# One graph, mixing and expert layer: order of the masked maxima, of three router items and of the last two row tiles changed

## The chip, the cores and the metric
The kernel runs on one core of a Trainium2 chip. The metric is the device time of one execution in microseconds (us). The core has five engines that run their own instruction lists and meet only through semaphores: TensorE (PE in the profile; PEld is its weight load), VectorE (DVE), ScalarE (ACT), GpSimd (POOL) and SyncE (SP), which here only issues transfers. GpSimd issues transfers too.

## The reference
1250 rows of 768 features go through a layer that sums three branches, and then through eight experts.

```
xn  = layernorm(x)
gnn = combined([layernorm(xn), out2]) @ Wu + bu
      out1 = gat_conv(., W1, 4 heads of 192);  out2 = gat_conv(out1, W2, 2 heads of 96)
mix = linear attention over random features of xn
x   = x + gnn + mix
x   = x + experts(layernorm(x)):  p = softmax(x @ router.T), the two largest p per row,
      divided by a balance that needs the sum of p over ALL rows, then renormalized;
      expert e: silu(x @ w1[e].T) @ w2[e].T, weighted and added per row
gat_conv, for every edge src -> dst, of 21,250:
      e = leaky_relu(s_src[src] + s_dst[dst]);  subtract the maximum over the edges of dst
      out[dst] = sum(exp(e) * h[src]) / sum(exp(e))
```

## The kernel before
The rows lie in NT = 10 tiles of 128. The edges are counted into a dense table `cnt` (source by destination), so each gat_conv is dense: for a head and a source tile (a **unit**), `attention` makes a row of 1280 scores for each of 128 sources. ScalarE writes the leaky branch into `vbuf` (L1025) from `u2_row`; VectorE adds `u1_row` and takes the larger into `pbuf` (`scores`, L1454); ScalarE takes exp (L1034); VectorE multiplies by the counts (L1466); TensorE multiplies by `h` (`aggregate`, L2008). `pbuf` has three buffers, so that `scores` of a unit waits for TensorE's end of the unit three before. The first attention has 4 heads, 40 units; the second has 2 heads, 20 units.

`u1_row` and `u2_row` of a head hold the maximum of each destination. They come about so: `mask` (ScalarE, L968) turns counts into a penalty `pen[dt]` for each destination tile; `masked_max` (VectorE, L1374: two instructions, the second reads the accumulator) takes the maximum over `a_row[h]` minus the penalty; `leaky_max` (L1382 to L1386) makes small columns `ucol`; TensorE turns them (`max_rows`, L1937, into bank `mT`); `maxima_rows` copies them (L1405); GpSimd writes them to DRAM (`maxima_out`, L711) and reads them back over all partitions (`rows_in_h`, L715 and L716, two transfers of 640 KB). These last two stand on GpSimd's queue in the order out 0, out 1, in 0, in 1. SyncE issues two weight loads (`w2g_raw`, `wuo`) as soon as the last tile of `h1` is done, which is about when GpSimd reads the rows of head 0.

For the second gat_conv VectorE takes the maxima of its 2 heads over 10 masks (20 `masked_max`). Beside them TensorE and ScalarE work on 12 router items (`PRE`: 10 row tiles and 2 pieces of a weight): six transposes (L2061, L2063), copies by ScalarE into `xp` (L1072), and six narrow products with the 8 router columns (L1770), read by ScalarE (L1079, L1081). `spread_rows(h)` (40 matmuls) spreads head h's columns and waits for VectorE's `m_done`. The order on TensorE is: items 0 to 6, spread 0, items 7 to 11, spread 1, second attention.

At the end each row tile t passes `residual(t)` on VectorE (L1536 to L1203), is stored to `out` by SyncE, gets its top two experts (`two_largest`, one group of tiles 0 to 6 and one of 7 to 9), is normalized on ScalarE (L1118) and stored to `early_d` and `y_d`. From the first group alone the first NE = 7 of the NS = 27 expert slots are filled. A slot's rows are gathered by GpSimd (L747, `xs`), which waits for `early_d` and for `rows_known`; TensorE turns them, ScalarE copies them (`turned`, L1135), and so on to the products and `yout` (L1160). The result is added to `out` by GpSimd's indirect transfer (L771), each of which waits for the one before. `importance` (TensorE) sums the probabilities of all tiles; `balances` and `gates` (VectorE) need it. ScalarE's list is fixed: normalize the first group, root and exponentials of the second, normalize the second (L1118), and only then `turned(0)`.

## Time and profile before
| | us |
|---|---|
| median of 3 runs | 1091.47 (1091.25 to 1094.06) |
| the profiled execution, its own time | 1085.47 |
| its span (first to last record) | 1083.7 |
| TensorE busy | 947.0 (87%) |
| VectorE busy | 667.2 (62%) |
| ScalarE busy | 427.8 (39%) |
| GpSimd busy | 386.6 (36%) |

The busy shares are means over stages with different limits, so that none of them tells what bounds a stage; the chain of work that ended last and the timeline do. A span of TensorE is modelled. PEclk is the share of full clock that was granted: 1.00 is 2.4 GHz and 0.50 is 1.2 GHz.

### The profile page before, as it was taken

What the parts mean: (1) busy time and instruction counts of PE and PEld (TensorE: products, weight loads), DVE (VectorE), ACT (ScalarE), POOL (GpSimd) and SP (SyncE); (2) the same over time, 40 slices, a digit from 0 to 9 for tenths busy, and PEclk for the clock granted to TensorE, in tenths of its full rate; (3) what the DMA queues carried; (4) which work ended last, traced back from release to release, by engine and by line L of the source; (5) the groups of instructions that cost most, each with busy time, mean ns of one, the idle gap of its engine ahead of it and who ended that gap; (6) DMA issues with size and microseconds to landing.
All of it is one profiled execution on the core that took longest, in us unless ns stands there. A gap on an engine that the chain in (4) does not pass through costs nothing.

```text
span 1083.7 us, 14577 instructions
## 1 busy us (share of the span) xinstructions
PE 947.0 (87%) x5216; PEld 809.1 (75%) x5216; DVE 667.2 (62%) x1635; ACT 427.8 (39%) x689; POOL 386.6 (36%) x298
## 2 busy tenths in 40 slices
PE   3999996999999993994889998999679659999992
PEld 3898754776779993994888898989677358777771
DVE  7769998312761321665999886875897876133330
ACT  2544103233430000446667786643883523322220
POOL 3158888888888881001000000000000012433331
PEclk9999998899999996998899999996899859999997
DMA  9995556432353469014001100057007492656653
GB/s 294 231 204 111 124 120 177 69 44 0 65 112 43 88 178 277 2 26 141 1 1 50 34 31 1 2 197 251 16 1 250 170 351 59 122 118 125 134 105 58
DMA packets 77891, 118.73 MB, mean 110 GB/s; under 512 B 32545, under 2 KB 51547, under 8 KB 77821
## 3 DMA queue, kind: packets, MB, share of 16 engines
q0 software_dynamic: 35344, 40.37, 22.1%
q1 hardware_dynamic: 42477, 77.44, 22.1%
q8 instruction: 43, 0.70, 0.3%
q14 instruction: 27, 0.22, 0.1%
HBM read 85.42 MB, written 32.35 MB: 109 GB/s over the span
## 4 chain that ended last, share of the span: by engine, by line
PE 23%; DMA 18%; DVE 12%; issue 6%; ACT 3%; POOL 1%; SPq 0%; POOLq 0%; DVEq 0%; ACTq 0%
PE bank L1770 15%; DMA out<-yout,sb_negq 13%; PE bank L2008 6%; DVE pbuf L1466 5%; DVE pbuf L1454 4%; DMA cnt<-table 3%; PE bank L1781 1%; ACT vbuf L1025 1%; DMA early_d<-x 1%; ACT h L1011 1%; DVE sb_before L1374 1%; PE bank L2061 1%; DMA u_row<-m_d 1%; DMA xs<-early_d,sb_negq 1%; POOL cnt L707 1%
## 5 line engine op out<-in xcount | busy, mean ns | idle before, releaser
L691 POOL DMA_INDIRECT table<-match_n,slot_ix x168 | 279.9, 1666 | 92.8 <-issue 48.8
L2008 PE MATMUL bank<-h,pbuf 128*128 128x193 f32 (+1 forms) x1200 | 189.9, 318 | 38.8 <-DVE pbuf L1466 35.8
L2008 PEld LDWEIGHTS bank<-h,pbuf 128*128 128x128 f32 x1200 | 180.7, 195 | 47.7 <-DVE pbuf L1466 43.4
L1374 DVE CUSTOM_DVE_ANT_0 sb_before<-a_row,pen 128x1280 bf16<-128x1280 f32 x60 | 89.3, 1489 | 17.7 <-ACT pen L968 12.8
L1238 DVE SCALAR_TENSOR_TENSOR junk_k<-keyrow,key,sb_before 128x384 uint8<-128x384 f32 x168 | 93.0, 615 | 10.3 <-DMA keyrow<-key_d 9.1
L747 POOL DMA_INDIRECT xs<-early_d,sb_negq x7 | 7.4, 1058 | 250.5 <-DMA early_d<-x 244.6
L1770 PE MATMUL bank<-xnT_hi,w_hi 128*128 128x512 f32 (+1 forms) x216 | 85.4, 395 | 12.6 <-issue 9.0
L1034 ACT ACTIVATE pbuf<-pbuf 128x1280 f32<-128x1280 f32 x60 | 76.6, 1277 | 41.2 <-DVE pbuf L1454 41.2
L1466 DVE SCALAR_TENSOR_TENSOR pbuf<-pbuf,cnt 128x1280 f32<-128x1280 f32 x60 | 88.7, 1483 | 0.0
L1770 PE MATMUL bank<-w_hi,xnT_hi 128*128 128x384 f32 x240 | 83.9, 350 | 0.0
L771 POOL DMA_INDIRECT out<-yout,sb_negq x27 | 43.5, 1613 | 112.1 <-DMA out<-yout,sb_negq 84.3
L1770 PE MATMUL bank<-w_hi,xnT_lo 128*128 128x384 f32 x240 | 82.3, 343 | 0.0
L1770 PE MATMUL bank<-w_lo,xnT_hi 128*128 128x384 f32 x240 | 82.1, 342 | 0.0
L1770 PE MATMUL bank<-xnT_lo,w_hi 128*128 128x512 f32 (+1 forms) x216 | 78.8, 365 | 0.0
L1770 PE MATMUL bank<-xnT_hi,w_lo 128*128 128x512 f32 (+1 forms) x216 | 78.3, 363 | 0.0
L1770 PE MATMUL bank<-w_all,hT 128*128 x216 | 76.7, 498 | 1.5 <-DVE hT L1755 1.5
L1454 DVE SCALAR_TENSOR_TENSOR pbuf<-u_row,sb_scol,vbuf 128x1280 f32<-128x1280 f32 x40 | 61.7, 1544 | 22.6 <-ACT vbuf L1025 15.5
L1770 PE MATMUL bank<-w_all,xT 128*128 x324 | 74.9, 382 | 0.0
L1770 PEld LDWEIGHTS bank<-w_all,xT 128*128 128x128 f32 x324 | 62.1, 192 | 13.9
L853 ACT ACTIVATE kq<-bank,sb_kqb_c 128x512 f32<-128x512 f32 (+1 forms) x36 | 22.2, 618 | 119.6 <-PE bank L1770 119.6
L1770 PEld LDWEIGHTS bank<-w_all,hT 128*128 128x128 f32 x216 | 39.2, 191 | 27.3 <-issue 3.3
L1770 PEld LDWEIGHTS bank<-xnT_hi,w_hi 128*128 128x128 f32 x216 | 41.8, 193 | 22.5 <-issue 16.5
(342 smaller groups left out, 1791.4 us busy)
## 6 DMA issues: line engine op xcount, KB each, us to landing
keyrow<-key_d SPq DMA_DIRECT2D x28, 384.0 KB, 3.7
cnt<-table POOLq DMA_DIRECT2D x20, 320.0 KB, 9.4
w_all<-in_w1T SPq DMA_DIRECT2D x8, 768.0 KB, 8.6
w_all<-in_w2T SPq DMA_DIRECT2D x8, 768.0 KB, 9.9
u_row<-m_d POOLq DMA_DIRECT2D x8, 640.0 KB, 6.0
w_raw<-in_kqvT SPq DMA_DIRECT2D x4, 1152.0 KB, 7.9
y_d<-x SPq DMA_DIRECT2D x10, 388.0 KB, 10.3
acc_d<-ubuf SPq DMA_DIRECT2D x20, 192.0 KB, 2.0
```

The lines of the kernel that those rows point to most:

```text
L691: pool.indirect_dma_start(table[i], bass.IndirectOffsetOnAxis(ap=slot_ix[:, g:g + 1], axis=0), match_n[:, g:g + 1], None, compute_op=ALU.a ...
L707: pool.dma_start(cnt[i][:, :], table_rows[1][r, :], accum_op=ALU.add).then_inc(cnt_in[i], 16)
L771: pool.indirect_dma_start(out, bass.IndirectOffsetOnAxis(ap=target[:, s:s + 1], axis=0), yout[s % YO][:, :], None, compute_op=ALU.add, bou ...
L853: step(nc.scalar.activation(kq[j % 2][0][:, 0:w], b[:, 0:w], ACT.Identity, bias=kqb_c[:, col:col + 1]))
L1011: ins = nc.scalar.activation(h1[:, t, h, 0:C1], b[:, o:o + C1], ACT.Copy, scale=rec1[:, t:t + 1])
L1034: nc.scalar.activation(pbuf[i % 3][:, :], pbuf[i % 3][:, :], ACT.Exp).then_inc(e_done, 1)
L1238: nc.vector.scalar_tensor_tensor(out=junk_k[g % 2][:, :], in0=keyrow[c % KR][:, w:w + KW * P], scalar=key[:, g:g + 1], in1=before[:, first ...
L1374: ins = nc.vector.tensor_tensor_reduce(out=junk_m[:, :], in0=rows_a[h][:, :], in1=pen_t[:, :], scale=1.0, scalar=-3e38, op0=ALU.subtract, ...
L1454: nc.vector.scalar_tensor_tensor(out=pbuf[i % 3][:, :], in0=u1_r[h][:, :], scalar=scol[:, h, st:st + 1], in1=vbuf[i % 2][:, :], op0=ALU.ad ...
L1466: nc.vector.scalar_tensor_tensor(out=pbuf[i % 3][:, :], in0=pbuf[i % 3][:, :], scalar=2.0, in1=cnt[st][:, :], op0=ALU.min, op1=ALU.mult).t ...
L1770: return nc.tensor.matmul(o, l, r, start=first, stop=last)
L2008: ins = nc.tensor.matmul(b[:, d * stride:d * stride + chans + 1], score[:, dt * P:(dt + 1) * P], h_t[:, st, h, 0:chans + 1], start=st == 0 ...
```

## The change
Five things move; no arithmetic changes.

1. Head 1's maxima over masks 4 to 9 are taken with head 0's, mask by mask. Head 2's move from the first attention to the place just ahead of it; head 3's move to units 4, 5, 7, 9, 11 and 13. Which `mT` bank and which TensorE place serve the rows follows from that.
2. GpSimd reads head 1's rows, and SyncE loads `w2g_raw` and `wuo`, only after head 0's rows have landed.
3. Router items 9, 10 and 11 move from the stage of the second maxima into the second attention.
4. `residual(8)`, `residual(9)` and the second group's variance move behind the first group's `rows_known`; `spare_places` moves ahead of `shifted(1)`. SyncE stores `early_d` ahead of the sums of tiles 8 and 9 and loads `w2` 0 and 1 when the last product of `fin` is done.
5. `importance` moves on TensorE behind the first two slots' first products.

```diff
-            for h in range(2):
-                for dt in range(4, NT):
-                    if h == 0:
-                        evacuated(dve, "pen", dt, 0), evacuated(dve, "pen", dt, 1)
+            for dt in range(4, NT):
+                evacuated(dve, "pen", dt, 0), evacuated(dve, "pen", dt, 1)
+                for h in range(2):
                     masked_max(pen[dt], a_row, (h,), dt)
-                leaky_max_1(h)
-                maxima_rows(h)
+            leaky_max_1(0), leaky_max_1(1)
+            for dt in range(4, NT):
+                masked_max(pen[dt], a_row, (2,), dt)
+                if dt in (6, 8):
+                    maxima_rows((dt - 6) // 2)
+            leaky_max_1(2)
+            maxima_rows(2)
...
-            for h, units in ((2, (1, 2, 4, 5, 7, 8)), (3, (10, 12, 14, 16, 18, 20))):
+            for dt, i in enumerate((4, 5, 7, 9, 11, 13), 4):
+                beside[i] = (lambda dt=dt: masked_max(pen[dt], a_row, (3,), dt),)
...
             finished(sp, "h1", 1, NT - 1)
+            sp.wait_ge(u_row_in[0], 32)
             sp.dma_start(w2g_raw[:, :, :], W2.rearrange("(k p) n -> p k n", p=C2)).then_inc(g_in, 16)
...
-            rows_in_h(0), rows_in_h(1)
+            rows_in_h(0)
+            pool.wait_ge(u_row_in[0], 32)
+            rows_in_h(1)
...
+            late = {}
+            for n, i in enumerate(range(PRE_IN_MAX, len(PRE))):
+                late[4 * n] = lambda i=i: pre_turned(i)
+                late[4 * n + 2] = lambda i=i: pre_logits(i)
+            aggregate("agg2", H1, H2, h2, S2, C2, 2, 5, late)
...
+            for n, i in enumerate(range(PRE_IN_MAX, len(PRE))):
+                late[4 * n + 2] = lambda i=i: pre_turned(i)
+                late[4 * n + 4] = lambda i=i: pre_out(i)
+            attention(H1, H2, u2_row_b, row_ready_2, {}, late)
...
             residual(GA)
             shifted(0)
-            residual(GA + 1)
             two_largest(0)
-            residual(GA + 2)
-            inv_std_begin(mv3, span(1))
             places(0)
...
             nc.vector.tensor_scalar(token_ix[:, 0:NE], row_f[:, 0:NE], -1.0, None, ALU.add).then_inc(rows_known, 1)
+            for t in range(GA + 1, NT):
+                residual(t)
+            inv_std_begin(mv3, span(1))
+            spare_places()
             shifted(1)
-            spare_places()
...
+            for t in range(GA + 1):
+                store_sum(t)
+            finished(sp, "fin", NT - 1, 1)
             load_w2(0), load_w2(1)
+            sp.wait_ge(row_done, 1)
+            for t in GROUPS[0]:
+                sp.wait_ge(y2_done, t + 1)
+                sp.dma_start(early_d[t * P:(t + 1) * P, :], x1[:, t, :]).then_inc(y_out[0], 16)
+            for t in range(GA + 1, NT):
+                store_sum(t)
...
             ranks(0)
             listing(0)
-            importance()
...
                     spare_rows()
+                    importance()
                     ranks(1)
```

VectorE, the end of head 1's maxima and the start of the first attention, before (`a_row_119` is head 2's row, `pen_127` the mask 4, `pbuf` and `vbuf` as above):

```order
L1382 TENSOR_TENSOR sb_mxc<-sb_mxc,sb_scol 128x10
L1383 SCALAR_TENSOR_TENSOR sb_mcol<-sb_mxc 128x10
L1385 TENSOR_TENSOR ucol<-sb_scol,sb_mcol 128x10
L1386 SCALAR_TENSOR_TENSOR ucol<-sb_scol,sb_mcol 128x10
L1405 COPY sb_srow<-bank 20x128
L1454 SCALAR_TENSOR_TENSOR pbuf_143<-u_row_133,sb_scol,vbuf_141 128x1280
L1454 SCALAR_TENSOR_TENSOR pbuf_144<-u_row_133,sb_scol,vbuf_142 128x1280
L1466 SCALAR_TENSOR_TENSOR pbuf_143<-pbuf_143,cnt_106 128x1280
L1454 SCALAR_TENSOR_TENSOR pbuf_145<-u_row_133,sb_scol,vbuf_141 128x1280
L1466 SCALAR_TENSOR_TENSOR pbuf_144<-pbuf_144,cnt_107 128x1280
L1374 ISA sb_before,sb_mxc<-a_row_119,pen_127 128x1280
L1374 ISA sb_mxc 128x1
```

VectorE at the same place of the changed kernel, up to the first attention's start:

```order
L1409 ISA sb_mxc 128x1
L1440 COPY sb_srow<-bank 20x128
L1409 ISA sb_before,sb_mxc<-a_row_119,pen_132 128x1280
L1409 ISA sb_mxc 128x1
L1417 TENSOR_TENSOR sb_mxc<-sb_mxc,sb_scol 128x10
L1418 SCALAR_TENSOR_TENSOR sb_mcol<-sb_mxc 128x10
L1420 TENSOR_TENSOR ucol<-sb_scol,sb_mcol 128x10
L1421 SCALAR_TENSOR_TENSOR ucol<-sb_scol,sb_mcol 128x10
L1440 COPY sb_mrow<-bank 20x128
L1491 SCALAR_TENSOR_TENSOR pbuf_143<-u_row_133,sb_scol,vbuf_141 128x1280
L1491 SCALAR_TENSOR_TENSOR pbuf_144<-u_row_133,sb_scol,vbuf_142 128x1280
L1503 SCALAR_TENSOR_TENSOR pbuf_143<-pbuf_143,cnt_106 128x1280
```

The maxima of head 2 (`a_row_119`; the last of its six, mask 9, is shown) now stand ahead of the first `scores` and no longer between the units; the copy of head 1's turned rows (`sb_srow`) stands behind its mask 8, the copy of head 2's behind its small columns.

TensorE, the end of the router items and the start of the second attention, before:

```order
L1770 MATMUL bank<-sb_rw_raw,xp_191 128x8 x6
L2061 MATMUL bank<-sb_ident,xa_187 128x128 x6
L1770 MATMUL bank<-sb_rw_raw,xp_190 128x8 x6
L2063 MATMUL bank<-sb_ident,wuo 128x96 x6
L1770 MATMUL bank<-sb_rw_raw,xp_191 128x8 x6
L2063 MATMUL bank<-sb_ident,wuo 128x96 x6
L1770 MATMUL bank<-sb_rw_raw,xp_190 96x8 x6
L1770 MATMUL bank<-sb_rw_raw,xp_191 96x8 x6
L1770 MATMUL bank<-sb_ident,ucol 128x128 x20
L2008 MATMUL bank<-h_154,pbuf_143 128x97 x10
L2008 MATMUL bank<-h_154,pbuf_144 128x97 x10
L2008 MATMUL bank<-h_154,pbuf_145 128x97 x10
```

TensorE at the same place of the changed kernel:

```order
L1807 MATMUL bank<-sb_rw_raw,xp_190 128x8 x6
L1807 MATMUL bank<-sb_ident,ucol 128x128 x20
L2046 MATMUL bank<-h_154,pbuf_143 128x97 x10
L2099 MATMUL bank<-sb_ident,xa_last 128x128 x6
L2046 MATMUL bank<-h_154,pbuf_144 128x97 x10
L2046 MATMUL bank<-h_154,pbuf_145 128x97 x10
L1807 MATMUL bank<-sb_rw_raw,sb_row_t 128x8 x6
L2046 MATMUL bank<-h_154,pbuf_143 128x97 x10
L2046 MATMUL bank<-h_154,pbuf_144 128x97 x10
L2101 MATMUL bank<-sb_ident,wuo 128x96 x6
L2046 MATMUL bank<-h_154,pbuf_145 128x97 x10
L2046 MATMUL bank<-h_154,pbuf_143 128x97 x10
```

Item 9 (`xa_last`) and item 10 (`wuo`) now stand behind units of `pbuf`; spread 1 (`ucol`, x20) follows item 8.

VectorE, from the entries of the first group (`rows_known` is raised by L1715) on, before:

```order
L1671 TENSOR_REDUCE sb_row_t<-col_hot 128x7
L1715 TENSOR_SCALAR sb_negq<-sb_row_t 128x7
L1185 RECIPROCAL sb_rs<-sb_sq 128x3
L1186 TENSOR_TENSOR sb_r<-sb_rs 128x3
L1187 TENSOR_TENSOR sb_r<-sb_r,sb_nt 128x3
L1188 TENSOR_SCALAR sb_r<-sb_r 128x3
L1189 TENSOR_TENSOR sb_rs<-sb_rs,sb_r 128x3
L1547 TENSOR_REDUCE sb_r<-sb_prob 128x3
L1548 TENSOR_TENSOR sb_prob<-sb_prob,sb_r 128x24
L1549 SCALAR_TENSOR_TENSOR sb_row_b<-sb_mv,sb_rs 128x3
L1551 TENSOR_TENSOR sb_prob<-sb_prob,sb_rs 128x24
L1675 TENSOR_SCALAR matches<-sb_wq,sb_row_b 128x128 x8
```

VectorE at that place of the changed kernel:

```order
L1707 TENSOR_TENSOR col_hot<-col_hot,sb_negq 128x560
L1708 TENSOR_REDUCE sb_row_t<-col_hot 128x7
L1749 TENSOR_SCALAR sb_negq<-sb_row_t 128x7
L1573 TENSOR_TENSOR x_162<-x_162,bank 128x384
L1576 TENSOR_TENSOR sb_prob<-bank,sb_row_b 128x8
L1573 TENSOR_TENSOR x_162<-x_162,bank 128x384
L1234 BN_STATS sb_stats<-x_162 128x6
L1235 BN_STATS sb_stats<-x_162 128x6
L1238 BN_AGGR sb_mv<-sb_stats 128x2
L1573 TENSOR_TENSOR x_162<-x_162,bank 128x384
L1576 TENSOR_TENSOR sb_prob<-bank,sb_row_b 128x8
L1573 TENSOR_TENSOR x_162<-x_162,bank 128x384
```

Two `residual` (of six instructions each) now stand between `rows_known` and the second group's root.

## Rows read from the trace of the kernel before

**Rows 1.** Busy time by stage: window, us, engines' busy us (instructions), PEclk, DMA share, GB/s

```profile
511.00:668.00 157.00, 141.73 (x834) 135.36 (x834) 139.37 (x139) 112.85 (x119) 5.57 (x14) 0.96 0.08 28
668.00:760.00 92.00, 85.54 (x656) 84.56 (x656) 63.82 (x211) 46.99 (x148) 0.00 (x0) 0.85 0.41 137
760.00:822.00 62.00, 47.46 (x367) 44.83 (x368) 58.65 (x44) 50.15 (x41) 0.00 (x0) 0.94 0.03 8
...
728.00:732.00 4.00, 4.00 (x22) 4.00 (x21) 3.78 (x9) 1.28 (x5) 0.00 (x0) 0.50 1.04 347
```

**Rows 2.** The chain that ended last: start us, us, what

```profile
504.03 7.42 DMA u_row<-m_d
...
868.31 10.51 DMA early_d<-x
879.71 7.02 DMA xs<-early_d,sb_negq
...
912.22 6.10 DMA out<-yout,sb_negq
```

**Rows 3.** Timeline of VectorE before the first attention: start, us, work [idle before, releaser]

```profile
485.39 1.49 DVE L1374 CUSTOM_DVE_ANT_0 sb_before<-a_row,pen 128x1280 bf16<-128x1280 f32 x1 [2.25 <-ACT pen L968]
...
489.15 1.49 DVE L1374 CUSTOM_DVE_ANT_0 sb_before<-a_row,pen 128x1280 bf16<-128x1280 f32 x1 [2.25 <-ACT pen L968]
...
502.38 0.28 DVE L1405 COPY sb_srow<-bank 20x128 f32<-20x128 f32 x1 [0.37 <-PE bank L1937]
```

**Rows 4.** Transfers issued in 570 to 600 us: count, KB each, us to landing

```profile
u_row<-m_d POOLq DMA_DIRECT2D x2, 640.0 KB, 5.6
```

**Rows 5.** Timeline of VectorE in the first attention, around one masked maximum

```profile
574.12 1.47 DVE L1466 SCALAR_TENSOR_TENSOR pbuf<-pbuf,cnt 128x1280 f32<-128x1280 f32 x1
575.52 1.47 DVE L1374 CUSTOM_DVE_ANT_0 sb_before<-a_row,pen 128x1280 bf16<-128x1280 f32 x1
576.93 0.07 DVE L1374 DVE_READ_ACCUMULATOR2_ANT sb_mxc<- 128x1 f32 x1
```

**Rows 6.** Timeline of TensorE in the first attention (x20 is one unit)

```profile
517.41 12.48 PE L2008 MATMUL bank<-h,pbuf 128*128 128x193 f32 x60 [15.07 <-DVE pbuf L1466]
...
613.49 30.45 PE L2008 MATMUL bank<-h,pbuf 128*128 128x193 f32 x180
```

**Rows 7.** Who waited for whom, 511 to 668 us: total us, times, longest

```profile
PE bank L2008 <- DVE pbuf L1466: 20.8, 11, 15.1
...
PE bank L2008 <- ACT h L1011: 2.6, 2, 1.5
```

**Rows 8.** Timeline of VectorE, second maxima's end and a `scores` of the second attention

```profile
746.96 0.17 DVE L1386 SCALAR_TENSOR_TENSOR ucol<-sb_scol,sb_mcol 128x10 f32<-128x10 f32 x1
...
776.23 1.54 DVE L1454 SCALAR_TENSOR_TENSOR pbuf<-u_row_b,sb_scol,vbuf 128x1280 f32<-128x1280 f32 x1
```

**Rows 9.** Timeline of TensorE: item 7, spread 1, a unit of the second attention

```profile
740.16 0.82 PE L2061 MATMUL bank<-sb_ident,xa 128*128 128x128 f32 x6
740.82 1.40 PE L1770 MATMUL bank<-sb_rw_raw,xp 128*128 128x8 f32 x12
...
752.17 7.37 PE L1770 MATMUL bank<-sb_ident,ucol 128*128 128x128 f32 x40
...
776.37 2.47 PE L2008 MATMUL bank<-h,pbuf 128*128 128x97 f32 x20 [0.39 <-DVE pbuf L1466]
```

**Rows 10.** Timeline of ScalarE, start of the second attention

```profile
759.89 2.61 ACT L1025 ACTIVATE vbuf<-u_row_b,sb_a 128x1280 f32<-128x1280 f32 x2
```

**Rows 11.** The chain that ended last, 760 to 775 us: TensorE's first unit there

```profile
765.87 4.60 PE bank L2008 x20
```

**Rows 12.** Timeline of VectorE in the routing

```profile
861.06 0.22 DVE L1581 TENSOR_TENSOR x<-sb_prob,sb_row_t 128x56 f32<-128x56 f32 x1
...
863.82 0.17 DVE L1590 COPY sb_row_b<-bank 128x8 f32<-128x8 f32 x1
...
878.52 0.17 DVE L1715 TENSOR_SCALAR sb_negq<-sb_row_t 128x7 uint32<-128x7 f32 x1
...
880.33 1.93 DVE L1675 TENSOR_SCALAR matches<-sb_wq,sb_row_b 128x128 f32<-128x128 f32 x8
```

**Rows 13.** Timeline of ScalarE in the routing

```profile
880.57 2.85 ACT L1118 ACTIVATE x<-x,sb_row_b,sb_rs 128x768 f32<-128x768 f32 x3
887.71 0.49 ACT L1135 ACTIVATE xT<-bank 128x384 f32<-128x384 f32 x1 [4.29 <-PE bank L1781]
```

More of the change, by code:

```diff
@@ L194, in gps_layer, with raw_at, raw_in, turned_at @@
         PRE = [("x", t) for t in range(NT)] + [("w", j) for j in range(2)]
-        PRE_FIRST = 7
+        PRE_FIRST, PRE_IN_MAX = 7, 9
+        xa.append(at("xa_last", 97600, [P, D]))
+        xp += [v[:, :].rearrange("p (k t) -> p k t", k=KD) for v in (accb, row_t)]
+        def raw_at(t):
+            return xa[t % XA] if t < PRE_IN_MAX else xa[XA]
+        def raw_in(t):
+            return xa_in[t % XA if t < PRE_IN_MAX else XA]
+        def turned_at(i):
+            return xp[i % 2] if i < PRE_IN_MAX else xp[2 + i % 2]
         consts = wq[:, :, :].rearrange("p k f -> p (k f)")
@@ L294, in gps_layer @@
         g_in, g_hi_done, g_split = sem("g_in"), sem("g_hi_done"), sem("g_split")
-        xa_in = [sem(f"xa_in{i}") for i in range(XA)]
+        xa_in = [sem(f"xa_in{i}") for i in range(XA + 1)]
         centred, shift_done = sem("centred"), sem("shift_done")
@@ L378, in gps_layer @@
                     reserve("mT", ROWS_AT[hf, t])
+        reserve("mT", 2)
         AGG = turn[0]
-        BESIDE = {0: [("b1T",), ("csum",)], 1: [("mT", 2)], 2: [("mT", 3)]}
+        BESIDE = {0: [("b1T",), ("csum",)], 1: [("mT", 3)]}
         for h in range(H1):
@@ L400, in gps_layer @@
         reserve("preT", 0, 0), reserve("preT", 0, 1)
-        for i in range(len(PRE)):
-            if i + 1 < len(PRE):
+        for i in range(PRE_IN_MAX):
+            if i + 1 < PRE_IN_MAX:
                 reserve("preT", i + 1, 0), reserve("preT", i + 1, 1)
@@ L407, in gps_layer @@
         reserve_spread(1)
-        for h in range(H2):
-            for i in range(2):
-                reserve("agg2", h, i)
+        AGG2 = turn[0]
+        for i in range(2):
+            reserve("agg2", 0, i)
+        for i in range(PRE_IN_MAX, len(PRE)):
+            for k, name in enumerate((("preT", i, 0), ("preT", i, 1), ("pre", i))):
+                reserve(*name, at_bank=AGG2 + 4 + k)
+        for i in range(2):
+            reserve("agg2", 1, i)
         reserve("o2T", 0)
@@ L419, in gps_layer @@
             reserve_fin(t)
-        reserve("rank", 0), reserve("list", 0), reserve("imp")
+        reserve("rank", 0), reserve("list", 0)
         def reserve_turned(s):
@@ L431, in gps_layer @@
             if s == 0:
-                reserve("spare"), reserve("rank", 1)
+                reserve("spare"), reserve("imp"), reserve("rank", 1)
             if s == 1:
@@ L635, in _ @@
                     sp.wait_ge(y2_done, t + 1)
-                    r = slice(t * P, (t + 1) * P)
-                    if g == 0:
-                        sp.dma_start(early_d[r, :], x1[:, t, :]).then_inc(y_out[0], 16)
-                for t in tiles:
-                    r = slice(t * P, (t + 1) * P)
-                    sp.dma_start(y_d[r, :], x1[:, t, :]).then_inc(y_out[1], 16)
+                    sp.dma_start(y_d[t * P:(t + 1) * P, :], x1[:, t, :]).then_inc(y_out[1], 16)
             sp.wait_ge(sum_out, 16 * NS)
@@ L1012, in bank_out, with attention @@
                 ins.then_inc(free("agg", h, i), 1)
-            def attention(h0, heads, u2_r, row_ready, out_at):
+            def attention(h0, heads, u2_r, row_ready, out_at, beside):
                 seq = [(h, st) for h in range(heads) for st in range(NT)]
@@ L1036, in attention @@
                         bank_out(h - 1, k)
-            attention(0, H1, u2_row, row_ready_1, {1: (0, 1), 2: (2, 3, 4)})
+                    if i in beside:
+                        beside[i]()
+            attention(0, H1, u2_row, row_ready_1, {1: (0, 1), 2: (2, 3, 4)}, {})
             act.wait_ge(g_in, 32)
@@ L1088, in _ @@
             pre_turned(0)
-            for i in range(len(PRE)):
-                if i + 1 < len(PRE):
+            for i in range(PRE_IN_MAX):
+                if i + 1 < PRE_IN_MAX:
                     pre_turned(i + 1)
@@ L1426, in small_columns @@
                                         ALU.add).then_inc(centred, 1)
-            beside = {3: (bias_row,), 6: (small_columns,), 9: (lambda: leaky_max_1(2),), 13: (lambda: maxima_rows(2),),
-                      21: (lambda: leaky_max_1(3),), 25: (lambda: maxima_rows(3),)}
-            for h, units in ((2, (1, 2, 4, 5, 7, 8)), (3, (10, 12, 14, 16, 18, 20))):
-                for dt, i in enumerate(units, 4):
-                    beside[i] = (lambda h=h, dt=dt: masked_max(pen[dt], a_row, (h,), dt),)
+            beside = {3: (bias_row,), 6: (small_columns,), 15: (lambda: leaky_max_1(3),), 19: (lambda: maxima_rows(3),)}
+            for dt, i in enumerate((4, 5, 7, 9, 11, 13), 4):
+                beside[i] = (lambda dt=dt: masked_max(pen[dt], a_row, (3,), dt),)
             def attention(h0, heads, row_ready, u1_r, stage, nbank, bank_out, out_at, behind_last, beside):
@@ L2081, in _ @@
             pre_turned(0)
-            for i in range(len(PRE)):
-                if i + 1 < len(PRE):
+            for i in range(PRE_IN_MAX):
+                if i + 1 < PRE_IN_MAX:
                     pre_turned(i + 1)
```

28 lines of the change are left out of this document (15 added, 13 removed).

## The prediction
> **What bounds the kernel now.** I read the page and the busy shares by stage first, then the chain that ended last, then the timeline of each engine in the four places that the change touches. The first attention (511 to 668 us) keeps TensorE at 141.7 of 157.0 us and VectorE at 139.4, so the two are nearly even and each hiccup of VectorE can become an idle of TensorE. In the second (760 to 822 us) VectorE is busy for 58.7 of 62.0 us and TensorE for 47.5: VectorE sets the pace [rows 1]. From 912 us on, 27 indirect additions to `out` hang on each other; the first that the chain shows starts at 912.22 us [rows 2], and 171.5 us remain to the end of the span (1083.7 less 912.2). The change touches nothing behind that point, so what comes earlier there comes earlier at the end, one to one. The chain names what releases each place ahead of it: the landing of head 0's rows (504.03 to 511.45 us), the stores of `early_d`, and the gathers that follow at 879.71 us [rows 2].
>
> **The change part by part.**
>
> *A, start of the first attention.* Before, VectorE sat idle for 2.25 us ahead of each of head 0's maxima over the last masks, waiting for the mask (485.39 and 489.15 us) [rows 3]. Head 1's maxima now go into these gaps: one `masked_max` takes 1.5 us. After the pair on mask 9 (489.15 + 2 x 1.53 = 492.2 us), two sets of small columns (2 x 0.85), five maxima of head 2 (5 x 1.53) and two copies of 0.28 us end at 502.1 us, against 502.66 us for the copy of head 1's rows before [rows 3]. GpSimd's queue goes on only after that copy (its out 1 stands ahead of in 0), so its reads of head 0 start 0.5 us earlier. Then the transfer: it took 7.42 us beside the two weight loads [rows 2]; two such transfers with nothing beside them landed in 5.6 us [rows 4]. The weight loads now wait, which gives 1.8 us. What is queued behind SyncE's new wait (`w2g_raw`, `wuo`) is wanted only after the first attention, and head 1's rows, behind GpSimd's, ten units later. VectorE's last work (mask 9 of head 2, small columns, copy) ends near 505 us, ahead of the landing near 509 us. A = -2.3 us; bounds -0.5 (no relief of the transfer) and -3.5.
>
> *B, length of the first attention.* On VectorE `scores` and the multiplication take 2.87 us a unit and a maximum adds 1.41 (576.93 less 575.52) [rows 5]; TensorE takes 30.45 / 9 = 3.38 us a unit [rows 6]. A unit with a maximum costs VectorE 4.28 us, 0.9 more than TensorE; one without gives back 0.5. Before, 12 maxima lay in units 1 to 20: 21 x 2.87 + 12 x 1.41 = 77.2 us of VectorE against 21 x 3.38 = 71.0 of TensorE, to which its slow first three units (12.48 less 10.1) [rows 6] and some 3 us of small products add 5.5: even, with no reserve. Now six remain, 68.7 us, and TensorE leads by 8. TensorE's idle in the stage, apart from the first wait of 15.1 us, is 20.8 - 15.1 = 5.7 us for VectorE's product and 2.6 us for ScalarE's bank copies at a head's end, 8.3 us in all [rows 7]. ScalarE's 2.6 us stay, as does part of VectorE's at the head changes and behind the six maxima; I keep 4.5 and take 3.8 away. B = -3.8; bounds -1.5 (only units 1, 2 and 5 profit) and -8.3 (all idle goes).
>
> *C, start of the second attention.* Head 1's small columns were ready at 747.13 us, but TensorE came to spread 1 only at 752.17 us, as items 7 to 11 stood ahead [rows 8, 9]. With only 7 and 8 there (7 starts at 740.16 and they end near 744), it waits for VectorE instead: spread 1 starts at 747.2 us. The spread takes 7.37 us as before [rows 9], and ScalarE's first `vbuf`, at 759.89 us [rows 10], comes at 755. C = -4.9; bounds -3.9 (the spread all at 1.2 GHz) and -6.5.
>
> *D, length of the second attention.* The three items return here. Each has transposes of 0.82 us and narrow products of 1.40 us [rows 9], less some overlap 0.7 and 1.3. TensorE has 0.39 us of idle a unit and starts the next `scores`' release about as much ahead of its need: VectorE's `scores` at 776.23 us needs a `pbuf` that TensorE left 0.3 us sooner [rows 8, 9]. So 0.7 us fits nearly into idle plus reserve; 1.3 us exceeds them by 0.5. The first transposes come while the clock is still low (a unit takes 4.60 us there [rows 11]) and cost 0.5 more. On ScalarE, 50.2 of 62.0 us busy [rows 1], a copy pair of 0.9 us delays the next `vbuf`, which has over 1 us of reserve since it is written a unit ahead; no cost. D = +0.5 + 3 x 0.5 = +2.0; bounds 0 and 3 x (0.82 + 1.40) = +6.7.
>
> *E, from the last `fin` products to the first experts.* Before, `two_largest(0)` had `residual(8)` ahead, and `places(0)` (863.82 us) had `residual(9)`, which took from 861.28 to 863.8 us, 2.5 us [rows 12]. Without them the picks of the first group end 2.1 us earlier (0.4 goes to a wait for ScalarE's exponentials), and 0.5 us more is saved at `places`, as TensorE's rank sums, hidden by `residual(9)` before, now show (I take 2.0 of 2.5 us). `rows_known`, 878.69 us before [rows 12], comes at 876.1. The stores of `early_d`, 10.51 us long among weight loads and `y_d` stores before [rows 2], no longer stand behind tile 9's store, and are down long before that. So the gathers start near 876.3 us instead of 879.71. But ScalarE copies turned rows only after the second group is normalized. VectorE must now do, from 876.1 us: two residuals (5.1), the spare places (1.93, moved ahead) [rows 12] and root and shift (1.9: 878.69 to 880.57 us [rows 12, 13]), so the exponentials come at 885.1 us and the three tiles (2.85 us [rows 13]) end at 888.0. Before, `turned(0)` started at 887.71 us [rows 13], released by the gather (7.02 us from 879.71 [rows 2]). The gain of 2.6 us in `rows_known` is spent: the gathers wait for ScalarE. `importance`, four short matmuls behind the first products, puts 0.3 us ahead of the first experts' second products, and `balances` and four slots' gates follow it on VectorE, some 2.6 us later than before, with about as much reserve. E = +0.5; bounds -2.6 and +3.5 (the second group's marks keep TensorE waiting in slot 1).
>
> Sum: -2.3 - 3.8 - 4.9 + 2.0 + 0.5 = -8.5 us. Against the profiled execution's own time, 1085.47 us, that is 1077.0. The median of the runs shown is 6.0 us longer than that execution; I take the same difference from it: 1091.47 - 8.5 = 1083.0 us.
>
> **A rule against the change.** The row first: in 728 to 732 us, among the router items, TensorE was busy for all of the 4 us and was granted 0.50, which is 1.2 GHz [rows 1]. So these items can go together with a low clock though the engine never rests. The Trainium skill (TensorE: Matmul & The Clock Gate, Part 4: PE-mode transpose) says that transposes do not count as busy for the clock gate as other matmuls do; by it the items could pull the clock down in the second attention. This trace agrees only in part: the attention's own stage was granted 0.94 [rows 1], and no run so far shows items inside it.
>
> **Rivals.** (1) *The moved items lower the clock in the second attention.* A unit at 1.2 GHz takes TensorE 4.60 us [rows 11] against the 2.87 at which VectorE paces it, +1.73 us. From seven low units on (+12.1, so +3.6 in all) the kernel is slower by more than 0.3%; with ten it is 1091.5 - 8.5 + 17.3 = 1100.3 us. For it speaks the row at 728 us; against it that between items there now stand two to four units of wide matmuls. 0.05.
> (2) *The gains of A to C are spent on the items and in the routing.* D at its bound (+6.7, every item on the path) and E at +3.5 (marks of the second group late): -11.0 + 10.2, 1090.7 us, no difference. Against it speaks TensorE's idle a unit; for it, that VectorE's block behind `importance` is now late. 0.10.
> (3) *Maxima out of the first attention give little*, since the head changes set the pace and keep their waits (2.6 us are ScalarE's [rows 7]): B = -0.5, 1086.3 us. 0.15.
> (4) *More is won:* B = -7 and the routing pays 1.5: 1077.8 us. 0.08.
> The forecast, 0.62.
>
> **How the numbers follow.** What a measurement of this kernel can tell from no change is about 0.3%, 3.3 us. Faster by more: the forecast, (3) and (4), 0.85; within: (2), 0.10; slower: (1), 0.05. The range leaves out (1) and most of (2), and takes in the bounds of B and D singly: 1076.5 to 1089.0 us.
>
> **What would show each step.** A: the first `vbuf` near 509 us and `u_row` landing in under 6 us. B: the first attention's products from first to last about 147 us long instead of 150.5, TensorE's idle without the first wait near 4.5 us. C: spread 1 released by VectorE's columns, about 3 us after item 8 ends. D: 62 to 64 us from the first `vbuf` to the last product of the second attention, and a granted clock of 1.00 after its first units. E: ScalarE's first `xT` copy released by its own normalizing, not by TensorE; GpSimd's second addition to `out` about 8 us earlier. It would be wrong if the clock falls between items, or if `rows_known` to the first `yout` grows by more than 5 us.

## The result, and the profile after

The changed kernel took 1078.21 us (median of 4 runs, 1072.82 to 1086.88) where the kernel before took 1092.63 us beside it (1091.25 to 1094.06): a ratio of 0.9881, with a 95% interval of 0.9835 to 0.9927, 1.2% faster. Two later comparisons gave 0.9887 [0.9842, 0.9933] and 0.9906 [0.9873, 0.9940]. The forecast was 1083.0 us, 8.5 us less than before; the runs show 10 to 14 us less. Ratios, intervals and ranges leave out runs of the chip's slower state, over 1.5% above the fastest of the same kernel (one of e2, one of e10); the medians are of all runs.

The profiled execution of the changed kernel is its longest of the four: 1086.88 us with a span of 1085.1 us, 1.4 us *longer* than the profiled span of before. So these two profiles alone would say "no gain". The reader must take them apart by stage, and beside further profiles of both kernels (e5 for the kernel before, e1 and e10 for the changed one). Each stage ends at a row that one can find in the timeline:

| stage, us | before | before, e5 | changed | changed, e1 | changed, e10 |
|---|---|---|---|---|---|
| start to the last mask's end | 489.0 | 488.7 | 492.6 | 488.5 | 488.9 |
| to the first `vbuf` (A) | 22.5 | 22.7 | 19.4 | 19.5 | 19.3 |
| to the first product | 5.9 | 5.9 | 6.2 | 6.2 | 6.2 |
| first attention's products (B) | 150.5 | 151.3 | 145.3 | 144.8 | 145.3 |
| to the rows ahead of the router items | 43.7 | 48.6 | 51.8 | 42.1 | 42.1 |
| to the second attention's first `scores` (C) | 49.8 | 56.3 | 46.5 | 48.1 | 46.5 |
| to its last product (D) | 64.5 | 64.5 | 65.3 | 65.5 | 65.3 |
| to the first scaled row `yout` (E, with 1.0 before it) | 76.1 | 75.9 | 77.7 | 78.4 | 76.9 |
| to the end of the span | 181.7 | 183.8 | 180.4 | 183.8 | 186.1 |

Three stages get shorter in every pair (A, B, C) and two longer (D, E). Two stages that hold nothing of the change (the fifth and the last) differ by up to 10 and 6 us between executions of the same kernel.

**Start of the first attention.** The changed kernel's chain of waits, then ScalarE's timeline (answers to [rows 2, 3]):

```profile
506.41 5.50 DMA u_row<-m_d
```

```profile
511.94 2.61 ACT L1053 ACTIVATE vbuf<-u_row,sb_a 128x1280 f32<-128x1280 f32 x2 [4.91 <-DMA u_row<-m_d]
```

The rows land in 5.50 us instead of 7.42. The last mask ended 3.54 us later than before in this execution, and still the first `vbuf` starts only 0.47 us later (511.94 against 511.47).

**The first attention.** Busy time from first to last product (window, us, engines, clock, DMA; answer to [rows 1]), and TensorE's waits in it (total us, times, longest; answer to [rows 7]):

```profile
518.13:663.46 145.33, 140.14 (x833) 134.79 (x833) 126.14 (x118) 107.18 (x115) 4.05 (x8) 0.99 0.09 29
```

```profile
PE bank L2046 <- DVE pbuf L1503: 15.2, 9, 10.5
```

Without the first wait 15.2 - 10.5 = 4.7 us of waiting are left, where it was 8.3 us. The line for ScalarE's bank copies (2.6 us in [rows 7]) is gone altogether.

**Between the attentions.** Four-microsecond windows of the changed kernel, first those behind the first attention, then TensorE's second attention from the timeline:

```profile
668.00:672.00 4.00, 3.07 (x14) 3.10 (x15) 2.89 (x12) 1.70 (x7) 0.00 (x0) 0.59 0.00 0
672.00:676.00 4.00, 4.00 (x20) 3.93 (x20) 1.07 (x8) 1.10 (x5) 0.00 (x0) 0.50 0.00 0
...
684.00:688.00 4.00, 4.00 (x21) 3.99 (x21) 1.39 (x6) 0.23 (x2) 0.00 (x0) 0.50 0.00 0
```

```profile
766.22 4.58 PE L2046 MATMUL bank<-h,pbuf 128*128 128x97 f32 x20 [6.32 <-DVE pbuf L1503]
770.59 1.09 PE L2099 MATMUL bank<-sb_ident,xa_last 128*128 128x128 f32 x6
771.52 4.80 PE L2046 MATMUL bank<-h,pbuf 128*128 128x97 f32 x40
776.15 1.43 PE L1807 MATMUL bank<-sb_rw_raw,sb_row_t 128*128 128x8 f32 x12
...
785.80 2.47 PE L2046 MATMUL bank<-h,pbuf 128*128 128x97 f32 x20 [0.39 <-DVE pbuf L1503]
```

TensorE is granted 0.50, 1.2 GHz, for some 20 us behind the end of the first attention, though it is fully busy from 669 us on. (Such a time at 0.50 is called a low stretch below.) That is why this execution is long: the stage took 51.8 us against 42.1 us in e1 and e10, where the same windows show 1.00. In the second attention the items stand between units as ordered, and from 772 us the clock is 1.00.

**Routing.** ScalarE's timeline (answer to [rows 13]):

```profile
885.70 0.22 ACT L1145 ACTIVATE sb_prob<-sb_prob 128x24 f32<-128x24 f32 x1 [1.78 <-DVE sb_prob L1588]
886.75 2.86 ACT L1153 ACTIVATE x<-x,sb_row_b,sb_rs 128x768 f32<-128x768 f32 x3 [0.83 <-DMA out<-x]
889.52 0.47 ACT L1170 ACTIVATE xT<-bank 128x384 f32<-128x384 f32 x1
```

The first `xT` copy stands directly behind ScalarE's own normalizing, which itself waited 0.83 us for the store of tile 9 to land. In e1 that wait was 1.84 us, and in e10 there was none:

```profile
875.31 2.86 ACT L1153 ACTIVATE x<-x,sb_row_b,sb_rs 128x768 f32<-128x768 f32 x3 [1.84 <-DMA out<-x]
```

### The profile page after: what moved, and what is told of

The parts are those of the page before. It is cut to its first block, busy times and chain, and to the rows that moved or that the text cites. A ratio compares the mean times of both kernels' runs of the same rounds, so it can differ in the third digit from the quotient of the medians.

```text
span 1085.1 us, 14578 instructions
## 1 busy us (share of the span) xinstructions
PE 956.8 (88%) x5216; PEld 818.8 (75%) x5216; DVE 668.2 (62%) x1635; ACT 426.6 (39%) x689; POOL 388.8 (36%) x298
## 4 chain that ended last, share of the span: by engine, by line
PE 34%; DMA 10%; DVE 9%; issue 4%; ACT 4%; POOL 2%; POOLq 0%; DVEq 0%; ACTq 0%; SPq 0%
PE bank L1807 22%; PE bank L2046 8%; DMA out<-yout,sb_negq 7%; DVE pbuf L1491 3%; DVE pbuf L1503 3%; DMA cnt<-table 2%; PE bank L1818 2%; ACT vbuf L1053 1%; ACT h L1039 1%; DVE sb_before L1409 1%; PE bank L2099 1%; ACT pbuf L1062 1%; POOL cnt L733 1%; PE bank L1983 1%; DMA out<-x 1%
## 5 line engine op out<-in xcount | busy, mean ns | idle before, releaser
L1807 PE MATMUL bank<-xnT_hi,w_hi 128*128 128x512 f32 (+1 forms) x216 | 85.9, 398 | 11.3 <-issue 7.6
L1807 PE MATMUL bank<-w_all,xT 128*128 x324 | 75.9, 385 | 3.6 <-ACT xT L1173 3.6
L1807 PEld LDWEIGHTS bank<-xnT_hi,w_hi 128*128 128x128 f32 x216 | 42.2, 195 | 21.3 <-issue 15.2
## 6 DMA issues: line engine op xcount, KB each, us to landing
w_raw<-in_kqvT SPq DMA_DIRECT2D x4, 1152.0 KB, 19.3
```

The lines of the kernel that those rows point to most:

```text
L1807: return nc.tensor.matmul(o, l, r, start=first, stop=last)
```

## The experiments

Times are medians beside those of the kernel before on the same chip: 1095.32 us for e1 to e4, 1095.65 for e5 to e8, 1093.55 for e9 to e12.

**e1, the changed kernel again.** No edit.

> The changed kernel a second time. In its first profiled execution TensorE was granted 0.50 from 672 to 688 us, behind its 8.1 us of idle at the end of the first attention, where the kernel before had it only for some 2.5 us, and again for most of the router items. Theory 'clock': how long the low clock lasts there differs from execution to execution and is no part of the change; this execution then shows another length (a low stretch of under 10 us behind 669 us in a median execution), steps A and B of the prediction (-3.1 and -5.2 us) stand as before, and the time lies 1.0 to 1.5% under the kernel before. Rival 'the change lowers the clock': the low stretch comes again at the same place with the same 20 us, and then the gain of 14 us in the timed runs must come from elsewhere, behind 700 us.

1081.07 us (0.9887). Behind the first attention the clock was 1.00 throughout and the stage took 42.1 us; A was -3.0 and B -5.7 us against the kernel before's first profile. Theory "clock" holds: the long low stretch does not belong to every execution of the changed kernel.

**e2, the three items back**; **e3, the routing back**; **e4, only the maxima moved.** Each is the changed kernel without, or the kernel before with, one part of the diff shown above:

```diff
-            for i in range(PRE_IN_MAX):
+            for i in range(len(PRE)):
...
             residual(GA)
             shifted(0)
+            residual(GA + 1)
             two_largest(0)
...
+            leaky_max_1(0), leaky_max_1(1)
```

The first piece is e2's, on the changed kernel; the second e3's, likewise; the third stands for e4, on the kernel before, with all hunks of the diff that name maxima or their units.

> The changed kernel with its three router items (tiles 8 and 9 and the weight columns 1) back ahead of spread 1. By the prediction (C -4.9, D +2.0) it is 2.9 us slower than the changed kernel, -5.6 us against the kernel before. Rival 'the move itself is worth nothing': with the low clock behind the first attention the columns of head 1 and the items end at about the same time, so it is equal to the changed kernel within 1.5 us. Rival 'the move is worth the whole surplus': the timed runs gained 14 us where 8.5 were forecast, so the move gives 8 us and this kernel gains only 6 us against the kernel before.

1088.09 us (0.9933 [0.9901, 0.9966]), 7.0 us slower than e1 by the medians, though the two intervals overlap: the rival "the whole surplus" fits in size. The stage itself says it more firmly. From the router's rows to the second `scores` it took 56.3 us, against 46.5 to 48.1 with the items moved and all else equal, 8.2 to 9.8 us more; the second attention took 64.5 us, 0.7 to 1.0 less. Not all else in this profile is the items' doing: its first attention and the stage behind it (148.7 and 45.4 us) had low stretches too.

> The changed kernel with the routing in the order of the kernel before (second group's residuals, spare places, importance, the stores of tiles 8 and 9). By the prediction (E +0.5) it is as fast as the changed kernel or 0.5 us faster. Rival 'the routing gives 2.6 us since ScalarE is no bound': it is 2.6 us slower. Rival 'the second group is late': it is 3.5 us faster.

1075.24 us (0.9846 [0.9796, 0.9897]), 5.8 us faster than e1 by the medians, more than any theory said, with overlapping intervals; see e9.

> The kernel before with only the moved maxima (pairs on the last masks, head 2 before the attention, head 3 in units 4 to 13); items, routing and the two waits on transfers as before. By the prediction (B -3.8, and of A the 0.5 us of the earlier copy, less 1.8 for the transfer that stays long) it gains 4.3 us; by the profile of the changed kernel (B -5.2) 5.7 us, with TensorE's idle without the first wait near 3 us. Rival 'head changes set the pace': 0.5 us for B, 1 us in all.

1092.74 us (0.9960 [0.9930, 0.9990]): 2.6 us, less than expected. The profile has 21.7 us from the last mask to the first `vbuf` (-0.7: the copy is 1.2 us earlier, but the transfer took 7.86 us) and 148.8 us for the products. This first attention had a low stretch of its own in the middle (windows of 0.65 and 0.50 from 20 to 28 us behind the first product), as e2 and e8 had, and e5 for half as long; it costs about 3.5 us (148.7 us in e2 against 145.3 in e10, the same code there). Less that, it is the changed kernel's length, and so are TensorE's waits in it:

```profile
PE bank L2012 <- DVE pbuf L1469: 17.2, 9, 12.5
```

Without the first wait 17.2 - 12.5 = 4.7 us are left, as in the changed kernel, and the wait for ScalarE's bank copies is gone here too. So the moved maxima alone give step B.

**e5, the kernel before again.** No edit.

> The kernel before, unchanged, for a second profile. The prediction took step C from a profile in which four of the five items behind the seventh ran at the full clock and the stretch from the first router rows (711.64 us) to the second attention's first scores (761.40 us) took 49.8 us. In two variants that keep the items there it took 56.3 us, with the items at a granted clock of 0.50. Theory 'lucky profile': here too it takes 54 to 57 us, and the span is over 1088 us. Rival 'the variants differ': it takes 50 us again, as the kernel before has the items at the full clock and only the moved maxima change that.

1099.56 us, span 1097.8. The stage took 56.3 us. Windows among its items, and TensorE's rows from the last items to spread 1:

```profile
737.00:741.00 4.00, 4.00 (x21) 4.00 (x20) 3.78 (x9) 1.43 (x4) 0.00 (x0) 0.50 0.79 243
741.00:745.00 4.00, 4.00 (x21) 4.00 (x21) 3.93 (x5) 1.27 (x4) 0.00 (x0) 0.50 1.08 357
...
761.00:765.00 4.00, 4.00 (x27) 4.00 (x26) 0.00 (x0) 0.77 (x4) 0.00 (x0) 0.50 1.03 411
```

```profile
753.96 0.82 PE L2061 MATMUL bank<-sb_ident,xa 128*128 128x128 f32 x6
...
760.84 3.90 PE L1770 MATMUL bank<-sb_rw_raw,xp 128*96 128x8 f32 x24
764.59 7.12 PE L1770 MATMUL bank<-sb_ident,ucol 128*128 128x128 f32 x40
```

VectorE's columns for spread 1 were ready at 753.83 us; five items stood ahead of it and it started 10.8 us later. In the profile that the prediction read, the delay was 5.0 us (747.13 to 752.17, [rows 8, 9]), since TensorE had been through the first seven items sooner: they took 17.9 us up to spread 0 (716.21 to 734.10) with only the last two at 1.2 GHz, against 23.1 us here (723.48 to 746.53); the rows ahead of them took 4.73 and 6.36 us. (The expectation put the fast items behind the seventh; it was those ahead of it.) Beside it the same rows of the changed kernel, e10 (VectorE's columns, then TensorE):

```profile
738.56 0.17 DVE L1421 SCALAR_TENSOR_TENSOR ucol<-sb_scol,sb_mcol 128x10 f32<-128x10 f32 x1
```

```profile
739.05 2.74 PE L1807 MATMUL bank<-sb_rw_raw,xp 128*128 128x8 f32 x24
741.65 4.71 PE L1807 MATMUL bank<-sb_ident,ucol 128*128 128x128 f32 x40
```

From the end of spread 0 to spread 1 it is 3.25 us (738.40 to 741.65) instead of 10.63 (753.96 to 764.59), 7.4 less, and spread 1 takes 4.71 us instead of 7.12, 2.4 less. Together that is the 56.3 - 46.5 = 9.8 us of the stage.

**e6, turned rows first.**

```diff
             exponentials(1)
-            normalized(1)
...
             turned(0), turned(1)
+            normalized(1)
             silu(0)
```

> The changed kernel with one thing moved on ScalarE: the copies of the first two slots' turned rows go ahead of the normalizing of the second group. Theory (step E of the prediction: the gathers wait for ScalarE, and normalizing waits up to 1.8 us more for the store of tile 9 to land): from the first product behind the attention to the first scaled output row it takes 72 to 73 us instead of 76.6, so 3 to 4 us less in all. Rival 'the clock takes it': the first products then run still more at the low clock (each 2.7 us instead of 1.4 us), and only 1 us is won. Rival 'second group late': gathers for the late slots come 1 us later and nothing is won.

1074.09 us (0.9804 [0.9768, 0.9841]), the lowest median; its interval lies below those of e1 and e10 and overlaps those of e3 and e9. ScalarE's timeline:

```profile
872.34 0.22 ACT L1145 ACTIVATE sb_prob<-sb_prob 128x24 f32<-128x24 f32 x1 [1.78 <-DVE sb_prob L1588]
872.47 0.47 ACT L1169 ACTIVATE xT<-bank 128x384 f32<-128x384 f32 x1
...
873.95 2.87 ACT L1153 ACTIVATE x<-x,sb_row_b,sb_rs 128x768 f32<-128x768 f32 x3
```

The copies stand right behind the exponentials. From the first product behind the attention to the first scaled row it took 72.8 us, 3.1 to 4.6 us less than the changed kernel's three profiles. The theory holds.

**e7, items as products** (on the kernel before).

```diff
-                            ins = nc.tensor.transpose(b[:, j * P:(j + 1) * P], xa[t % XA][:, c], ident[:, :])
+                            ins = mm(b[:, j * P:(j + 1) * P], xa[t % XA][:, c], ident[:, :], True, True)
```

> The kernel before with the router items' transposes done as ordinary products with the identity. The Trainium skill (TensorE: Matmul & The Clock Gate, Part 4: PE-mode transpose) says that transposes do not count as busy for the clock. Theory 'transposes lower the clock': among the items the granted clock stays at 1.00 (it was 0.50 for 20 us of them in e1 and e4), the stretch from the router rows to the second scores takes 50 us or less. Rival 'narrow products lower it too' (12 products of 8 columns an item): the clock falls all the same and the stretch takes 56 us or more, since an ordinary product of this size is no shorter than a transpose (0.12 and 0.14 us).

1092.34 us (0.9979 [0.9944, 1.0015]). The same windows of the items as in e5, and a pair of an item's rows:

```profile
728.00:732.00 4.00, 4.00 (x37) 4.00 (x37) 3.90 (x7) 1.34 (x4) 0.00 (x0) 1.00 0.60 166
736.00:740.00 4.00, 4.00 (x38) 4.00 (x38) 3.93 (x5) 1.34 (x4) 0.00 (x0) 1.00 0.64 174
```

```profile
725.71 1.58 PE L1770 MATMUL bank<-sb_ident,xa 128*128 128x128 f32 x12
727.13 1.40 PE L1770 MATMUL bank<-sb_rw_raw,xp 128*128 128x8 f32 x12
```

All seven items before spread 0 run at 1.00, though the narrow products stayed as they were. An item costs 2.7 us (starts 725.71 and 728.39) against 3.7 us as transposes at 1.2 GHz (starts 727.71 and 731.44 in e10) and 1.95 us as transposes at full clock (starts 742.08 and 744.02 in the kernel before). Behind them, at the last items and spread 1, the clock fell all the same (0.50), so the stage took 53.5 us, between the two guesses, and of its 2.8 us nothing certain reached the time.

**e8, fillers** (on the changed kernel): `warm(16, "w2", 0)`, `warm(16, "aR", 0, 0)` and `warm(48, "agg2", 0, 0)` at the three places, with

```diff
+            def warm(n, *name):
+                b = take(pe, *name)
+                for _ in range(n):
+                    mm(b[:, 0:P], ident[:, :], ident[:, :], True, True)
```

> The changed kernel with unused products of 128 columns (identity by identity, into a bank that is overwritten later) in three of TensorE's idles: 16 behind the first transposes of the attention's output (idle 2.2 us), 16 before the router's rows (2.1 us), 48 before the second attention (6.3 us). Theory 'idles lower the clock': the low stretch behind the first attention (2 to 20 us long so far) and that of the second attention's first unit (4.6 us instead of 2.5) are gone; 2 to 3 us are won for sure and up to 9 in executions in which the first was long. Rival 'the clock falls behind the idle that stays' (1.3 us, or the items): nothing changes, or the fillers add up to 2 us as they run at the low clock and end late.

1083.85 us (0.9888 [0.9852, 0.9925]), slower than e1's 1081.07 by less than the intervals tell apart. The last filler:

```profile
751.43 10.88 PE L1807 MATMUL bank<-sb_ident 128*128 128x128 f32 x96
762.15 1.03 PE L2046 MATMUL bank<-h,pbuf 128*128 128x97 f32 x8
```

I had sized them by half their length: each product stands as two records of 0.113 us, and 48 ran 10.9 us into an idle of 6.3. The first product of the second attention came 8.7 us behind the first `scores` instead of 4.5. But the clock was 1.00 in all ten windows of four microseconds behind the first attention and in the first six of the second.

**e9, routing back again; e10, the changed kernel a third time.** No new edit.

> The changed kernel with the routing of the kernel before, a second time. Its first profile had only 0.7 to 1.4 us less than the changed kernel from the first product behind the attention to the first scaled row (75.96 against 76.64 and 77.39 us), but its timed runs lay 5.8 us lower. Theory 'E is a term of +1 to 2 us': beside a third run of the changed kernel it is 1 to 2 us faster, and the rest was clock and DMA luck in six runs. Rival 'the routing order costs 5 us': it is 5 to 6 us faster again, and the profile shows it behind the first scaled row, in the chain of additions.

> The changed kernel a third time, to stand beside the others of this call: 1077 to 1082 us. From the router rows to the second scores 46 to 48 us, with the last items of that stretch at a granted clock of 0.50.

e9: 1076.35 us (0.9848 [0.9816, 0.9880]). e10: 1083.74 us (0.9906 [0.9873, 0.9940]; 1072.84 to 1088.89). The timed runs speak for the rival (7.4 us, where e3 had 5.8). The two profiled executions (1077.55 and 1078.27 us) do not show it: from the last mask to `yout` no stage differs by over 0.12 us, from the first product behind the attention to the first scaled row they took 75.8 and 75.9 us, and the chain of additions, where the rival looks, is 1.1 us shorter with the old order (172.5 against 173.6 us). What of the new routing order costs 5.8 and 7.4 us in the medians of timed runs is not in these profiles.

**e11, items as products on e6; e12, e11 with 9, 8 and 24 fillers.** The edits are those of e7 and e8.

> The changed kernel with the copies of the turned rows first (as in e6) and all router items' transposes as ordinary products. In e7 that kept the clock at 1.00 among seven items and cost 0.7 us an item. Theory 'the clock now holds up to spread 1': spread 1 starts as soon as the columns of head 1 are there (0.2 us behind them instead of 2.9) and runs at the full clock (4.7 us), so the stretch from the router rows to the second scores takes 43 to 44 us against 46.5; the items in the second attention cost VectorE-paced units nothing more. 2 to 3 us under e6 (1074): 1071.5. Rival 'the clock falls later instead' as it did in e7 behind the seventh item: then the low stretch meets spread 1 and nothing is won.

> e11 with unused products in the three idles, now of a length that fits (each took 0.234 us in e8): 9, 8 and 24 of them instead of 16, 16 and 48. Theory: second attention's first scores to its first product goes back to 4.5 us (8.7 in e8), its unit at the full clock saves 1.3 to 2 us, and the waits in front of the output's products and the router's rows are not longer than in the changed kernel; 2 to 3 us under e11. Rival: fillers only shift where the clock falls (in e8 it fell among the items), and the first attention's middle or the routing's start takes a low stretch instead; equal to e11.

e11: 1076.05 us (0.9854 [0.9813, 0.9895]). Spread 1 started 0.05 us behind its columns and the stage took 45.3 us, 1.2 less; but the clock fell under spread 1 (6.4 us) and the second attention took 67.1 us, 1.8 more than with transposes. Nothing won against e6 (1074.09). e12: 1077.25 us (0.9855 [0.9828, 0.9882]), all six runs from 1075.50 to 1077.72. TensorE's rows around the second attention's start:

```profile
741.95 7.55 PE L1807 MATMUL bank<-sb_ident,ucol 128*128 128x128 f32 x40 [2.33 <-DVE ucol L1421]
749.34 5.52 PE L1807 MATMUL bank<-sb_ident 128*128 128x128 f32 x48
755.82 1.36 PE L2046 MATMUL bank<-h,pbuf 128*128 128x97 f32 x10 [0.96 <-DVE pbuf L1503]
```

The filler now fits, the first unit runs at 1.00 and the second attention takes 64.7 us; from the last mask to `yout` e12 needed 395.0 us, the least of all profiles (398.1 in e6). But its masks ended at 493.9 us and its end, behind `yout`, took 187.0 us. The low stretch moved to spread 1 (7.55 us); the rival had a shift, but named other places.

## Why the prediction was right, step by step

**A (-2.3 us): right in cause, a little small.** Measured -3.0 to -3.4. The copy that GpSimd waits for comes 1.2 us earlier relative to the last mask (13.4 us behind it before, 12.2 us after), where 0.5 was forecast; the transfer gives 1.9 us where 1.8 was forecast. e4, with neither of the two new waits, has the long transfer and gains only 0.7 us. That is inside the bound of -3.5. Which of the two waits gives the 1.9 us is not shown: in the kernel before, the weight loads ran beside head 0's rows until 508.46 us, and GpSimd's reads of head 1 from 508.95 us on until head 0's landed at 511.45.

**B (-3.8): right in cause, mis-sized.** Measured -5.2 to -6.5, within the bound of -8.3. TensorE's idle fell to 4.7 us (4.5 forecast), but not in the way described: ScalarE's 2.6 us, which I kept, went, and 4.7 of VectorE's 5.7 stayed. A further 1.6 us is busy time (141.73 against 140.14 us). The low clock at the stage's start ended 3.8 us behind the first product instead of 4.8; at half speed that is 0.5 us (an estimate from these two), and the other 1.1 us is not explained. e4 shows that the maxima alone bring the idle time down.

**C (-4.9): the step that was mis-sized, outside its bounds.** Measured -3.3 against the profile that the prediction read, but -9.8 against e5. The step set the gain by VectorE's columns (747.13 us), since in the one profile TensorE would have been there first without the three items. With the items in place three profiles of four (e2, e4, e5) had 56.3 us; only the one at hand had 49.8. Where the first seven items run at 1.2 GHz, TensorE is the late one: then all 7.4 us of the moved items come off, and spread 1 is faster as well. So in the changed kernel too TensorE came 1.8 to 2.9 us after the columns and did not wait for them. The sum was made against a lucky execution: its stage was 6.5 us shorter than that of e2, e4 and e5. The prediction saw that the whole execution lay 6.0 us under the median and added these 6.0 us to before and after alike, but a surplus in this stage is what the change takes away. With 9.8 in place of 4.9 the forecast would have been 1078.1 us, against 1078.21 measured; as it stood it was 4.8 us too high, and it held because the range reached down to 1076.5.

**D (+2.0): right in sign.** Measured +0.7 to +1.0. The items fit into TensorE's idle between units but for the first one. Rival 1, by which they would pull the clock down, is refuted: in all nine profiles with the items there the clock was 1.00 from at most 6 us behind the second attention's first product to its last. The mark for D was misread: 62 to 64 us from the first `vbuf` to the last product could not come out, as the stretch was 66.0 us long before the change (759.89 to 825.91; the window of 760 to 822 us ends too soon). It is 66.8 us now.

**E (+0.5): the chain as forecast, the size inside its bounds.** The gathers start 50.0 us behind the first product (e10: 864.48 less 814.48) where it was 52.8 us (879.71 less 826.92), 2.8 us earlier for 2.6 forecast; and the first `xT` copy is released by ScalarE's normalizing, 60.5 us behind it in e10 against 61.1 forecast. What was not in the sum: the normalizing waits for tile 9's store, which now is issued behind those of `early_d` (0.8 and 1.8 us in two of three profiles), and the first experts' products spent more of their time at 1.2 GHz (7.06 us for 24 against 6.09). Measured +0.8 to +2.5 against the kernel before. Not all of this is the new order's: e3 and e9, which differ from the changed kernel in the routing alone and keep the old order, took 76.0 and 75.8 us, as much as e10 (75.9). Only what the other two profiles have above it, 0.7 and 1.5 us, goes with the new order, and it is about the wait for tile 9's store. From `rows_known` to the first `yout` it takes 3.6 to 5.1 us more than in the first profile of before; e1 (28.4 against 23.3 us) just passes the 5 us that the prediction named as a sign of being wrong. e6 shows that this ordering, not the gathers, is what holds the gain back: 3 to 4.6 us come out as soon as the copies no longer stand behind the normalizing. GpSimd's second addition, expected 8 us earlier, came 2.75 us *later* in the first profile (914.97 against 912.22) and near 900.6 us in e10: a mark on an absolute time tells nothing when single executions differ by 10 us.

**The remainder.** That what comes earlier at 912 us comes earlier at the end one to one was too simple: the 27 additions took between 168.3 and 174.7 us from the first to the last in the fourteen profiles, by how fast each lands.

The sum of the mean differences in the table is -11.3 us (A -3.2, first product +0.3, B -5.8, C -6.0, D +0.8, E +1.7, and +0.9 in stages without an edit). Put e5's C of 9.8 us in place of the mean, and it is -15; the timed runs say 10 to 14.

**The clock rule.** The row first: items as transposes ran at a granted 0.50 with TensorE busy for all of each window (e5), and the same items as products at 1.00 (e7). The Trainium skill (TensorE: Matmul & The Clock Gate, Part 4: PE-mode transpose) says that transposes do not count as busy as other products do; by that rule the trace of the first seven items agrees. The same section of the Trainium skill also says that the full clock does not engage for them; there the measurement decides: in the kernel before, items 7 and 8 ran as transposes at 1.00, six in 0.82 us, before the clock fell at 744 us. And it is not the whole of it: in e7 the clock fell at the last items and in e11 and e12 under spread 1, where all were products. It did not speak against this change but for it: taking such items out from ahead of spread 1 took off 9.8 us against e5, where 4.9 were forecast.

**Left open.** Why the routing's new order costs 5.8 and 7.4 us in the medians of timed runs but 0 to 1.6 us in the profiles: the wait on tile 9's store varies, and e6, which takes the normalizing behind it off the path, has neither the cost nor the wide spread (1070.96 to 1077.52 in six runs against 1072.84 to 1088.89 in ten of e10), but no profile caught a wait long enough. Also why the clock stayed at 1.00 behind the first attention in eight of nine profiles with the items moved, and in none of the five with the items in place, when that stage comes ahead of the items.

## What to carry to other kernels

Take a stage's price from more than one profile before you put it into a sum, above all where it holds transposes or follows an idle of TensorE: the same move was worth 3.3 us against one execution and 9.8 against three others. A difference between that execution and the median is not the same before and after, if it lies in a stage that the change touches. When a move shortens a chain on one engine, look at which in-order engine the chain meets next and what stands ahead there; the gain of the earlier gathers lay behind one normalizing on ScalarE, and one moved line brought it out. Fillers must be sized by measured records, and they moved the low stretch more than they won time; that they steady a kernel is not shown (its runs spread over 2.2 us in e12, but over 7.8 in e8, and over 6.6 in e6 without any).

## What the runs showed of the hardware

- Behind the same two waits of 1.3 and 2.2 us around short transposes TensorE was granted 1.2 GHz for 20.5 us in one execution of the changed kernel and not at all in two others: 51.8, 42.1 and 42.1 us for the same stage.
- A router item of 6 transposes and 6 products of 8 columns took 3.7 us at 1.2 GHz and 1.95 at 2.4 GHz; with ordinary products in place of transposes 2.7 us, at 2.4 GHz.
- With unused products in the idles of the second attention's start its first unit of 20 products ran at 1.00 from the first product on (e12: 2.47 us); without them it took 4.58 us.
- Beside two weight loads and, for its last 2.5 us, the reads of the next head's rows the landing of head 0's rows took 7.42 us; with neither beside it 5.50 us.
